# GpSimd's lead over TensorE counted in whole pairs of groups, in the first two sums of a graph network

## What is computed

```python
def rgcn(x, W, SW, b):                       # W: 8 relations x 128 x 128
    xt = einsum('nd,rde->rne', x, W)
    agg = segment_sum(xt[rel, src], dst, num_segments=12500)
    return relu(agg + x @ SW + b)

y = rgcn(rgcn(x, w1, sl1, b1), w2, sl2, b2)  # sums one and two
x = layernorm(x + y)
feat = relu(x @ W1 + b1)
h = feat * d_invsqrt                         # d: edges per destination
agg = segment_sum(h[src], dst, num_segments=12500)   # sum three
out = layernorm(x + (feat - agg * d_invsqrt) @ W2 + b2)
```

## Time and profile before

| | |
|---|---|
| three runs | 7330.13, 7333.13, 7347.31 us |
| profiled execution, its own time | 7344.55 us |
| its span, first to last instruction | 7342.5 us |
| busy: GpSimd, TensorE, VectorE, ScalarE | 4716.7, 3401.5, 1715.6, 689.9 us |
| the DMAs of sum one, first to last start | 4.5 to 2444.2 us |
| of sum two (after the first 14, on L780) | 2480.2 to 4912.8 us |
| of sum three (after the first 21, on L780) | 4968.6 to 7323.7 us |

### The profile page before, as it was taken

The page is one execution under the profiler, slowest core; times in us unless marked ns, Lnnn a source line. Parts: engine busy times, 40 slices in busy tenths (PEclk is TensorE's granted clock), DMA queues, the critical chain, the costliest instruction groups (busy, mean ns, idle before and its releaser), DMA issues.

```text
span 7342.5 us, 56548 instructions
## 1 busy us (share of the span) xinstructions
PE 3401.5 (46%) x15692; PEld 3003.5 (41%) x15693; DVE 1715.6 (23%) x2832; ACT 689.9 (9%) x1395; POOL 4716.7 (64%) x4992
## 2 busy tenths in 40 slices
PE   3554544545455545545555555454333333333333
PEld 3544444444444444444444444444333333333333
DVE  4433333333333212222222222211111111111111
ACT  2111111111111111111111111110000000000000
POOL 6666666666666566666666666655666666666665
PEclk7666666666666666666666666765555555555555
DMA  2111111111111111111111111111111111111111
GB/s 63 48 51 50 50 50 50 53 50 49 51 52 50 47 47 55 57 56 54 55 57 56 55 57 54 58 52 44 51 53 50 51 52 51 52 51 51 51 52 49
DMA packets 197664, 382.88 MB, mean 52 GB/s; under 512 B 84402, under 2 KB 93406, under 8 KB 197622
## 3 DMA queue, kind: packets, MB, share of 16 engines
q0 software_dynamic: 159456, 326.88, 15.5%
q1 hardware_dynamic: 36496, 54.67, 2.1%
q10 hardware_dynamic: 1670, 0.85, 0.0%
HBM read 356.43 MB, written 25.65 MB: 52 GB/s over the span
## 4 chain that ended last, share of the span: by engine, by line
issue 27%; POOL 26%; another core or an unknown queue 24%; PE 15%; DVE 4%; DVEq 2%; DMA 1%; ACT 0%; POOLq 0%; ACTq 0%; SPq 0%
POOL rows L806 26%; PE bank L989 6%; PE bank L964 6%; DVE r_S L1054 2%; PE bank L1222 1%; DVEq L1083 1%; DMA rows<-h_d,idx 1%; DVE r_hot L1049 1%; DVE acc L1093 1%; PE bank L1607 1%; PE bank L1593 0%; DMA rows<-x_d,idx 0%; PE bank L1386 0%; DMA acc<-in_dst_dram 0%
## 5 line engine op out<-in xcount | busy, mean ns | idle before, releaser
L806 POOL DMA_INDIRECT rows<-in_x_dram,idx x1661 | 1573.7, 947 | 869.6 <-issue 539.6
L806 POOL DMA_INDIRECT rows<-x_d,idx x1647 | 1555.3, 944 | 893.0 <-issue 537.6
L806 POOL DMA_INDIRECT rows<-h_d,idx x1640 | 1553.7, 947 | 819.1 <-issue 517.6
L989 PE MATMUL bank<-r_S,rows 128*128 128x128 f32 x6644 | 1265.2, 338 | 1371.6 <-issue 1293.8
L989 PEld LDWEIGHTS bank<-r_S,rows 128*128 128x128 f32 x6644 | 1132.4, 247 | 1493.4 <-issue 1491.1
L1222 PE MATMUL bank<-r_S,rows 128*128 128x64 f32 x3322 | 775.0, 416 | 1425.7 <-DMA rows<-h_d,idx 973.0
L1222 PEld LDWEIGHTS bank<-r_S,rows 128*128 128x128 f32 x3322 | 738.3, 328 | 1473.1 <-issue 909.6
L1054 DVE TENSOR_TENSOR r_S<-bank,key 128x1792 f32<-128x1792 f32 x238 | 480.1, 2017 | 869.0 <-remote 737.8
L917 ACT COPY r_agg<-bank 128x512 f32<-128x512 f32 x476 | 277.7, 583 | 3907.4 <-remote 3053.1
L964 PE MATMUL bank<-r_agg,w2s 128*128 128x128 f32 x1920 | 509.7, 414 | 242.0 <-issue 215.3
L964 PE MATMUL bank<-r_agg,w1s 128*128 128x128 f32 x1920 | 506.6, 417 | 239.1 <-issue 170.4
(11 more groups left out here) (150 smaller groups left out, 1343.8 us busy)
## 6 DMA issues: line engine op xcount, KB each, us to landing
rows<-in_x_dram,idx POOLq DMA_INDIRECT x1661, 3.4
rows<-x_d,idx POOLq DMA_INDIRECT x1647
rows<-h_d,idx POOLq DMA_INDIRECT x1640
d_xr<-in_x_dram SPq DMA_DIRECT2D x54, 218.0 KB
x_d<-d_yr SPq DMA_DIRECT2D x27, 218.0 KB
d_x1r<-x_d SPq DMA_DIRECT2D x27, 218.0 KB
h_d<-d_hr SPq DMA_DIRECT2D x27, 218.0 KB
part_d<-d_pr SPq DMA_DIRECT2D x27, 218.0 KB
```

The source lines that it names most:

```text
L806: pool.indirect_dma_start(out=self.c.rows[:, self.place(s), :], out_offset=None, in_=self.table[:, :], in_offset=bass.IndirectOffsetOnAxis ...
L989: mm = pe.matmul(agg_ps[j][:, bass.ds(offs[j * KG + k], TK)], c.rows[:, g.place(h * KG + k), :], S[:, pb, j * KG + k, :], start=False, sto ...
```

## The change

In sums one and two, from pair 12 on, the boundary of pair p now waits for both groups of pair p-2, and the wait in the middle of the pair is gone. The leads of passes 0 to 2, the mix by pairs and all of sum three stay as they are.

```diff
                 pool.wait_ge(self.idx_ready, (q * (IT + 1) + i) * PR + p + 1)
-                short = self.incs - 1 if lead == NEAR else 0
-                pool.wait_ge(self.summed, self.pairs_summed(q, i, p + PR - lead) - short)
+                pool.wait_ge(self.summed, self.pairs_summed(q, i, p + PR - lead))
                 if ahead_of is not None and p in ahead_of:
                     pool.wait_ge(*ahead_of[p])
                 gate(pool, self.c.passed)
                 for h in range(p * PAIR, (p + 1) * PAIR):
-                    if short and h % PAIR:
-                        pool.wait_ge(self.summed, self.pairs_summed(q, i, p + PR - lead))
-                        gate(pool, self.c.passed)
                     for k in range(part.of(h)):
```

## The result

The changed kernel takes 7399.73 us (median of 6 runs, 7377.43 to 7418.18) against 7336.16 us before (6 runs, 7325.85 to 7352.33): a ratio of 1.0083, with a 95% interval of 1.0070 to 1.0097. It is slower by about 61 us. The sign and the moved wait as its cause were forecast, at 141 us; the time lies inside the range, but the size is less than half of what was said. The profiled execution has a span of 7391.6 us, 49.1 more than before.

A forecast was written before the change was run, and what follows sets the result against it. GpSimd's gathers were taken to bound the kernel. 143 stops at 5.36 us, 767 us, less the 625.5 us of now gave +141 us; 7333.13 + 141 = 7474 us, 1.9% slower, range 7240 to 7610 us.

The forecast's parts named there:

- What bounds the kernel: GpSimd's gathers, one every 1.25 us, bound all three sums; its stops, 325 and 341 us in sums one and two, can move.
- Instructions taken out at 0: Mid-pair in sums one and two: removing one wait and one increment for each pair changes the time by 0 us.
- The number of stops: GpSimd's stops in sums one and two: 143 forecast, midway between 112 and 175.
- sum three's rate: Sum three, already under the new rule, stops 56 times in 107 boundaries, 112 for two sums; -25 us at that count.
- the sum taken one by one: Sums one and two, nothing given back: 157 + 66 + 24 = +247 us, with 175 boundary stops (125 + 16 + 34).
- The price of a stop: Each GpSimd stop in sums one and two: 4.1 + 1.26 = 5.36 us, 767 us for 143 stops.
- The stretch of 1.26 us: At 125 boundary stops, waiting for the second group's increment adds 157 us, 1.26 us each; bounds 86 and 228 us.
- TensorE's rows at 0: TensorE's gathered rows land a few us later after a stretched stop; one whole pair in the ring covers it, 0 us.
- the upper end of the range: 7610 us; the case if the ring's cover were gone, TensorE idled and its groups were done later still.
- The 34 middle stops: Mid-pair stops, 115 us, go, but 4.1 us at each boundary replaces them: +24 us, bounds -115 and +63 us.
- Sum three's balance comes over: Rival, faster: sums one and two get sum three's stops, 282 us each; 101 us less, 7232 us; chance 0.23.
- It all comes out even: Rival: TensorE's work sets the stops' total in sums one and two, so no change, 7333 us; chance 0.13.

The follow-up runs named there:

- e4: The changed kernel's boundary wait for both groups of pair p-2, but the wait and increment in the middle kept: 7403.76 us, ratio 1.0096 to the kernel before.
- e11: The change itself measured again beside the kernel before: 7460.84 us against 7376.49, ratio 1.0107.
- e1: The change made in sum one alone, against the kernel before: 7366.14 us against 7337.27, ratio 1.0045.
- e2: The change made in sum two alone, against the kernel before: 7385.90 us, ratio 1.0062.
- e3: The kernel before with only the wait in the middle of the pair removed, boundary wait as before: 7368.98 us, ratio 1.0049.
- e16: The changed kernel with only 2 of the 8 relations in the mix of sums one and two: 6250.23 us, the kernel before 6256.66.
- e15: The kernel before, old waits, with only 2 of the 8 relations in the mix of sums one and two: 6250.58 us, the kernel before 6256.66.
- e5: The changed kernel's boundary wait, plus a middle wait for the first group of pair p-1: 6260.29 us, ratio 1.0004 to the kernel before.
- e10: The same kernel as e5, run again: 6275.10 us, the kernel before 6271.39, ratio 1.0004.
- e6: The kernel before with a lead of three whole pairs in sums one and two: 6257.15 us, ratio 0.9998.
- e9: The same kernel as e6, run again: 6272.26 us, the kernel before 6271.39, ratio 1.0002.
- e13: Three whole pairs of lead in sums one and two, as e6, tried again: 6256.33 us, the kernel before 6256.66.
- e17: Three whole pairs of lead in sums one and two, as e6, third try: 6259.62 us, the kernel before 6259.44.
- e18: The changed kernel with 2 of the 8 relations in the mix, as e16, in another set: 6251.74 us, the kernel before 6259.44.
- e7: The kernel before with only the ring's own limit, four pairs of lead, in sums one and two: 6257.61 us, ratio 0.9999.

## Why the prediction was right or wrong

*What bounds the kernel*: right. 44 of the 49 us that the profile gained stand before gathers of GpSimd.

*Instructions taken out at 0*: right, by e4 (they stay there and the time is that of the change).

*The number of stops*: right. 143 was forecast, midway between sum three's rate and the 175 of the sum taken one by one, and 143 were counted (73 and 70); e4 has 140, e11 148. The midpoint was a choice and not a derivation, and sums with the same code differ by up to nine stops, so the exact hit is luck.

*The price of a stop*: wrong, and this is the step that failed. The text put 4.1 + 1.26 = 5.36 us on all 143, 767 us; the measured mean is 665.2 / 143 = 4.65 us, 102 us less in all. That is +41 us against the 624.5 of before, where +141 was said, and GpSimd's idle time rose to 786.0 and 825.5 us, not to 840 and 860. The stretch of 1.26 us was an average over 125 boundary stops of very different kinds, most of them (82) with the second copy within 1.34 us of the first, and was then laid on every stop. The runs show in its place two kinds of stop with prices of their own. Where TensorE's records of the awaited group were done, the stops did not stretch: 3.62 us before, 3.72 now. Where they were not, they last 6.67 us, and there are 45 of these instead of 20. By length the picture is similar, 2.76 to 2.92 us for the short stops and 4.92 to 6.09 for the long ones, and taking the 1.26 us off the 65 short ones would lower the forecast by 82 us, to +59, beside +61 measured. That agreement is not a proof. The sorting by length was made after the result, and long does not mean that TensorE was still at work: in 34 of the 78 long stops of the change the awaited group's records were done. The same change cost 84 us in e11.

*TensorE's rows at 0*: not as it was said. The text held one whole pair in the ring to be cover enough, and named over 100 us of waiting for rows a sum as a sign of being wrong. It is 196.0 and 166.4 us, in e1, e2, e4 and e11 too wherever the stricter boundary stands (144 to 198 us a sum), and 8.8 to 62.9 where it doesn't. The text went on that the upper end of the range would then be the case, and that did not come: the kernel loses 61 us. How much of the 61 us goes back to these waits no run separates; that more groups are not done when GpSimd falls silent fits them.

*The 34 middle stops, +24 us with bounds from -115*: the sign was right. e3 points the same way: with them gone and nothing made stricter the kernel loses 32 us, and the boundaries have 19 stops more. Here the lower bound, that an earlier stop makes them superfluous, is excluded for this kernel in this condition.

*Most of it in sum two*: not said, and should have been, from 64 us of stretch there against 22 in sum one. One of its wide stops, at pair 73, has a step of the tail between the two groups; that this is the reason in general was not tried.

*The rivals.* "Sum three's balance comes over" fell: sums one and two have 143 stops, not 112. "It all comes out even" fell where increments are late (e1, e2), and holds where they are not, as far as e16 against e15 shows it (0.35 us). The rule of the Trainium skill that was set beside it (Perfetto Trace Analysis, section Tensor Engine Instruction: the increment is sent when the accumulator memory has acknowledged, and is then visible to all) agrees with e5 to e10, where the copy starts 0.04 us after the record's end. In the profile of before the same distance is 8 us in the median and up to 28; since the record's end is modelled, this can't tell a late acknowledgement from a late increment, but the rule taken together with the recorded ends does not hold there. The text gave the latter the decision, and was right for the runs that count here, but took for the kernel's nature what is a condition of its surroundings.

*Not settled*: why TensorE's increments are late in some sets of runs and not in others, and whether it goes by the chip, what in GpSimd's silence brings them out, and whether the sum of the stops depends on TensorE's work or on a longer lead. Each attempt at the last two (e6, e9, e13, e17; e15, e16, e18) met the condition without stops. That silence causes the release is read from the order of events at the stops and was not tried by itself.

## What to carry to other kernels

When a wait is moved to a later event, do not multiply a mean stretch by the number of waits: sort the waits first by what the producer has done when the wait begins. Here those with the awaited work done kept their length (3.62 and 3.72 us), and the loss came with those in which it was not. A wait that stops the bounding engine can be worth keeping, since removing it alone cost 32 us here. A cover that is costed at 0, such as the rows in the ring, is to be read again after the change. And before tuning how closely one engine may follow another, measure the unchanged kernel on several occasions: the whole effect of these waits was seen only in one of two conditions, in which the same program takes 7337 or 6257 us.

## What the runs showed of the hardware

- ScalarE's copy, which waits for TensorE's semaphore increment, started up to 28 us after the modelled end of the matmul's record in some sets of runs (the kernel before: 7336 to 7376 us, profile of the first set) and 0.04 us after it in others (6257 to 6271 us, profile of e7). A whole set was in one of the two, three sets in the first and four in the second, without regard to the kernel, and no chip that the record names was in both.
- In the first condition TensorE's records also come slowly at times, one in 0.7 to 2.8 us where the usual distance is 0.11 or 0.21. In the kernel before 808 distances from one record's start to the next on L989 are of 0.6 to 0.8, 1.2 to 1.6 or 2 to 2.9 us; in e7, where the line is L990, one.
- In that condition TensorE started 0.6 to 0.7 matmul records per us around the moment in which GpSimd stopped issuing gathers, and about 4 per us from 5 us after it (137 stops of the change, 152 of the kernel before).
- GpSimd's gather took the same in both, 944 ns in the median in the kernel before and in e7.
